# The last gated MLP on its selected rows alone: count, gather, compute, scatter

## What is computed

```python
def _L1_ffn_ref(x, attention_mask, wr, br, w1, b1, w2, b2):
    weights = (jnp.einsum('bsd,do->bso', x, wr) + br)[..., 0]
    k = max(1, int(CAPACITY * s))
    kk = k - 1 if k > 1 else 1
    _, idx = jax.lax.top_k(weights, k)
    sel_idx = idx[:, :kk]
    sel = jnp.take_along_axis(x, sel_idx[:, :, None], axis=1)
    h = jax.nn.gelu(jnp.einsum('bkd,dh->bkh', sel, w1) + b1)
    y = jnp.einsum('bkh,hd->bkd', h, w2) + b2
    w_sel = jnp.take_along_axis(weights, sel_idx, axis=1)
    y = y * w_sel[..., None]
    processed = jnp.zeros_like(x).at[batch_idx, sel_idx].set(y)
    return processed + x
...
x = x + _L1_ffn_ref(_layernorm(x, axis=-1)[None], ...)[0]
```

## Time and profile before

| | before |
|---|---|
| median of 3 runs, us | 9628.36 (9627.92 to 9630.96) |
| the profiled execution, us | 9602.17, of it a span of 9600.4 |
| norm3, from its first instruction to select's, us | 8602.9 to 8731.7 |
| select, us | to 8812.9 |
| ffn1, us | to 9560.6 |
| store, us | to the end of the span |

### The profile page before, as it was taken

One profiled execution on the slowest core, in us unless ns is written; L12 is line 12 of the kernel. 1 busy time (PEld: TensorE's weight loads), 2 busy tenths in 40 slices (PEclk: granted clock), 3 DMA queues, 4 the chain that ended last, 5 costly groups with the idle time before them and its releaser, 6 DMA issues. The chain is left out here.

```text
span 9600.4 us, 124500 instructions
## 1 busy us (share of the span) xinstructions
PE 6901.1 (72%) x33680; PEld 5343.1 (56%) x33681; DVE 3347.4 (35%) x5992; ACT 1650.1 (17%) x3477; POOL 4866.2 (51%) x6031
## 2 busy tenths in 40 slices
PE   2687776777756799766887888100498887886998
PEld 2544444555436576634666666100488886566886
DVE  4111113444323423333445454107333324992000
ACT  0123330000001122211222222000012332011221
POOL 1566657778772000476777777760365333651000
PEclk9898778899875899688889888655699998986999
DMA  4665555555432000356666666561689998861002
GB/s 147 230 201 176 182 171 186 170 170 173 128 91 80 25 20 22 128 186 199 198 200 199 201 196 201 184 189 35 191 285 305 305 305 280 277 215 56 17 19 65
DMA packets 724617, 1585.81 MB, mean 165 GB/s; under 512 B 135844, under 2 KB 442523, under 8 KB 691281
## 3 DMA queue, kind: packets, MB, share of 16 engines
q1 hardware_dynamic: 429272, 785.42, 24.5%
q0 software_dynamic: 206080, 553.05, 20.1%
q10 hardware_dynamic: 89115, 245.78, 7.0%
HBM read 1098.27 MB, written 487.90 MB: 165 GB/s over the span
## 5 line engine op out<-in xcount | busy, mean ns | idle before, releaser
L893 POOL DMA_INDIRECT rows_ring<-h_rows,src_idx x1660 | 1668.2, 1005 | 757.6 <-issue 474.2
L2627 POOL DMA_INDIRECT rows_ring<-x_rows,src_tile x1573 | 1543.3, 981 | 496.0 <-issue 432.0
L2290 PE MATMUL agg_ps_z<-agg_wt,agg_rows 128*128 128x110 f32 x8640 | 1043.3, 285 | 148.4 <-DVE agg_wt L2251 51.4
L2290 PEld LDWEIGHTS agg_ps_z<-agg_wt,agg_rows 128*128 128x128 f32 x8640 | 1027.4, 201 | 164.6 <-issue 164.4
L1014 PE MATMUL agg_ps_sum<-rows_ring,agg_sel_w 128*128 128x257 f32 x1960 | 645.9, 474 | 288.1 <-DMA rows_ring<-h_rows,src_idx 160.3
L2238 POOL DMA_DIRECT2D agg_rows<-tile_rows x864 | 465.8, 541 | 591.6 <-PE agg_ps_z L2290 522.0
L977 DVE TENSOR_TENSOR agg_sel<-iota,dst_item 128x640 bf16<-128x640 f32 x332 | 274.0, 825 | 916.3 <-PE agg_ps_sum L1015 647.7
L1014 PEld LDWEIGHTS agg_ps_sum<-rows_ring,agg_sel_w 128*128 128x128 f32 x1960 | 341.2, 218 | 445.1 <-issue 358.3
L1014 PE MATMUL agg_ps_sum<-agg_rows,agg_sel_w 128*128 128x257 f32 x1360 | 432.5, 462 | 153.9 <-issue 101.1
L2903 PE MATMUL mix_ps_h<-mix_x1t,mix_w 128*128 128x256 f32 x1600 | 395.6, 404 | 17.7 <-issue 8.5
L2912 PE MATMUL mix_ps_f<-mix_w,mix_ht 128*128 128x256 f32 x1600 | 389.0, 398 | 0.9 <-issue 0.9
(11 more groups left out here) (590 smaller groups left out, 12277.9 us busy)
## 6 DMA issues: line engine op xcount, KB each, us to landing
tile_rows<-rows_ring SPq DMA_DIRECT2D x121, 1696.5 KB
agg_rows<-tile_rows SPq DMA_DIRECT2D x1296, 128.0 KB
agg_rows<-tile_rows POOLq DMA_DIRECT2D x864, 128.0 KB
agg_rows<-edge_rows SPq DMA_DIRECT2D x68, 1290.0 KB
edge_rows<-rows_ring ACTq DMA_DIRECT2D x65, 1290.0 KB
z_sums<-agg_z ACTq DMA_DIRECT2D x98, 660.0 KB
fin_z<-z_sums SPq DMA_DIRECT2D x98, 660.0 KB
xn_turned<-norm_xt SPq DMA_DIRECT2D x200, 256.0 KB
```

The lines of the kernel that those rows point to most:

```text
L893: pool.indirect_dma_start(self.ring[:, lot % LOT_RING, i, :], None, self.table, bass.IndirectOffsetOnAxis(g.src_idx[:, item:item + 1], 0)) ...
L2290: mm = pe.matmul(ps[:, bass.ds(off + c * CW, CW)], rows[:, u, i, c * P:(c + 1) * P], wt[:, u, i, :, :].rearrange("p a b -> p (a b)"), star ...
L2627: pool.indirect_dma_start(self.ring[:, s, i, :], None, g.x_rows, bass.IndirectOffsetOnAxis(g.src_tile[:, tile:tile + 1], 0)).then_inc(self ...
```

## The change

The phases norm3, select, ffn1 and store become router, select and ffn1.

- **router** has no transposes and no matmul. DVE scales a group (two tensor_scalar) and then makes the router weight of each tile itself, by a scalar_tensor_tensor of `xn` and `wr` (both in SBUF) with the row sum as its accumulator output, two to a group. POOL adds `xn` into `x_sb` as before. SP stores the normalized group, and ACT stores x + n of the group, side by side into a DRAM table `slot_rows` (2 KB for each node: n in the first half, x + n in the second).
- **select** gets the seven stores of `x_sb` to the output, on SP, at its start. After the choice is made it builds tables: PE turns the 0/1 marks to one row for each tile, DVE scans them, and PE sums over tiles, so that `slot_counts` holds for each node how many are chosen up to it. For each of 6400 slots (`SEL_TILES` = 50 tiles of 128) DVE finds the tile that holds it, with a comparison of 128 x 5000 elements and a reduction over them.
- **ffn1** runs over 25 groups of slots, written out without a loop. POOL gathers, two indirect DMAs each for a group: the row of counts of each slot's tile, from which DVE counts the node (`find`); and that node's 2 KB row. PE transposes the group (4 transposes, `turn`), DVE copies it out of PSUM (`keep`) and makes the router weight again (`weigh`), PE and ACT do the MLP as before, DVE makes the result rows (`finish`), and POOL scatters them over the output by two indirect DMAs (`give`). Slots past the 6249th get a node number beyond the output, and their rows are dropped.
- store and `g.gain` are gone.

The core of the diff, cut:

```diff
@@ router (new) @@
+                for gi in range(GROUPS):
+                    u = gi % SLOTS
+                    if gi >= SLOTS:
+                        dve.wait_ge(rows_out[u], 16 * (gi // SLOTS))
+                        dve.wait_ge(added, gi + 1 - SLOTS)
+                        dve.wait_ge(weighed, GROUP * (gi + 1 - SLOTS))
+                    for j in range(GROUP):
+                        t = gi * GROUP + j
+                        dve.tensor_scalar(xn[:, u, j, :], g.x_sb[:, t, :], mean[:, t:t + 1], rstd[:, t:t + 1], ALU.subtract, ALU.mult).then_inc(scaled, 1)
+                    dve.wait_ge(scaled, GROUP * (gi + 1))
+                    if gi:
+                        dve.wait_ge(weighed, GROUP * gi)
+                    for j in range(GROUP):
+                        t = gi * GROUP + j
+                        dve.scalar_tensor_tensor(junk[:, j, :], xn[:, u, j, :], 1.0, wr[:, :], ALU.mult, ALU.mult,
+                                                 accum_out=g.router[:, t:t + 1]).then_inc(weighed, 1)
...
+                for gi in range(GROUPS):
+                    act.wait_ge(added, gi + 1)
+                    act.dma_start(table[gi, :, :, C:2 * C], g.x_sb[:, gi * GROUP:(gi + 1) * GROUP, :]).then_inc(base_out, 16)
...
+                    pool.wait_ge(scaled, GROUP * (gi + 1))
+                    at = g.x_sb[:, gi * GROUP:(gi + 1) * GROUP, :]
+                    pool.tensor_tensor(at, at, xn[:, gi % SLOTS, :, :], ALU.add).then_inc(added, 1)
...
+                    sp.wait_ge(scaled, GROUP * (gi + 1))
+                    sp.dma_start(table[gi, :, :, 0:C], xn[:, u, :, :]).then_inc(rows_out[u], 16)
@@ select @@
+                for a, b in zip(cuts[:-1], cuts[1:]):
+                    sp.dma_start(to[:, a:b, :], g.x_sb[:, a:b, :]).then_inc(stored, 16)
+                sp.dma_start(g.out[FULL_TILES * P:NODES, :], g.x_sb[0:TAIL, FULL_TILES, :]).then_inc(stored, 16)
+                sp.wait_ge(counts_ready, 1)
+                sp.dma_start(g.sel_counts, counts[:, :]).then_inc(stored, 16)
...
+                wide = [P, SEL_TILES, TILES]
+                done(dve.tensor_tensor(passed[:, :, :], ends[:, :].unsqueeze(1).to_broadcast(wide), g.slot_no[:, :].unsqueeze(2).to_broadcast(wide), ALU.is_le))
+                done(dve.tensor_reduce(tile_f[:, :], passed[:, :, :], AX, ALU.add))
@@ ffn1, POOL @@
+                def ask_counts(gi):
+                    s = gi % SEEN
+                    if gi >= SEEN:
+                        pool.wait_ge(found, gi - SEEN + 1)
...
+                def ask_rows(gi):
+                    s = gi % HELD
+                    pool.wait_ge(found, gi + 1)
+                    if gi >= HELD:
+                        pool.wait_ge(added, gi - HELD + 1)
...
+                        pool.indirect_dma_start(rows[:, s, j, :], None, g.sel_rows, bass.IndirectOffsetOnAxis(row_at[:, k:k + 1], 0)).then_inc(held[s], 16)
...
+                def give(gi):
+                    s = gi % OUT
+                    pool.wait_ge(added, gi + 1)
...
+                ask_counts(0)
+                ask_counts(1)
+                for gi in range(N):
+                    if gi + 2 < N:
+                        ask_counts(gi + 2)
+                    ask_rows(gi)
+                    if gi >= 3:
+                        give(gi - 3)
+                for gi in range(N - 3, N):
+                    give(gi)
@@ ffn1, PE @@
+                turn(0)
+                for gi in range(N):
+                    u = gi % 2
+                    pe.wait_ge(kept, gi + 1)
+                    for i in range(4):
...
+                    if gi + 1 < N:
+                        turn(gi + 1)
+                    if gi:
+                        last(gi - 1)
+                last(N - 1)
@@ ffn1, DVE @@
+                find(0)
+                find(1)
+                dve.wait_ge(w_loaded, 96)
+                keep(0)
                 b2.split(dve, g)
+                weigh(0)
+                for gi in range(N):
+                    if gi + 2 < N:
+                        find(gi + 2)
+                    if gi + 1 < N:
+                        keep(gi + 1)
+                        weigh(gi + 1)
+                    if gi:
+                        finish(gi - 1)
+                finish(N - 1)
```

More of the change, by code:

```diff
@@ L77 @@
 KEEP = NODES // 2 - 1
+SEL_TILES = -(-KEEP // (2 * P)) * 2
 TERMS = GAT_HEADS + 1
@@ L3208, in _, with turn @@
             @block.tensor
             def _(pe):
-                pe.wait_ge(w_loaded, 64)
-                pe.wait_ge(b2.ready, 1)
-                def last(gi, u, first):
+                pe.wait_ge(w_loaded, 96)
+                def turn(gi):
+                    pe.wait_ge(held[gi % HELD], 16 * GROUP * (gi // HELD + 1))
+                    if gi:
+                        pe.wait_ge(kept, gi)
+                    for j in range(GROUP):
+                        for c in range(KC):
+                            mm = pe.transpose(ps_t[:, c, j * P:(j + 1) * P], rows[:, gi % HELD, j, c * P:(c + 1) * P], g.ident[:, :])
+                    mm.then_inc(turned, 1)
```

261 lines of the change are left out of this document (186 added, 75 removed).

## The result

The changed kernel takes **9229.0 us** (median of 4 runs, 9227.5 to 9279.1), the kernel before 9629.7 (4 runs, 9627.9 to 9647.0): ratio 0.959, 95% interval 0.9571 to 0.961. The prediction was 9282 with a range of 9238 to 9328.

The account below looks back on a forecast made before the run. PE was taken to bound ffn1 from end to end; -382.4 (ffn1 and store) + 14.8 (tables) + 21.7 (router) = -345.9 us, taking the median 9628.4 to 9282.5 us, range 9238 to 9328.

Parts of the forecast that it names:

- What bounds, and the halved work: ffn1: PE stays the bound, 25 groups replace 50, and ffn1 with store falls from 787.5 to 405.1 us, gain 382.4.
- first result: ffn1: 14.8 us of start, then 25.7 us from first matmul to first result, 40.5 us in all.
- 22 periods of 15.23: ffn1: each group costs today's 14.63 us plus 0.6 for four transposes; 22 such periods make 375.6 us.
- The start: ffn1's start: POOL's eight indirect DMAs (9.8 us), landing 2.6, transposes 1.1, copy 0.7 and waits 0.6 make 14.8 us.
- The store: Seven output stores beside select: their 39.8 us fit into its 81.2 us without DMA, so cost nothing.
- The tables: select's end: a serial chain with two long operations of 5.3 us each, cost 14.8 us, range 13 to 20.
- Router: router for norm3: POOL's addition holds DVE's second sum, period 2.85 us, stage 150.5 us against 128.8, cost 21.7.
- A: router: no contention, DVE's sums run beside POOL's addition, period 2.0 us, 42 us less, total 9241; chance 8%.
- B: ffn1: a handover in each group costs 1 to 2 us more, 25 to 50 in all, 9308 to 9333; chance 13%.
- C: ffn1: run-ahead fails, gathers asked for only when due, 30.9 us a group, 392 us more, 9675; chance 2%.
- D: ffn1: work not halved, as slots past the choice were many, near 9650 with the tables' cost; under 1%.
- The carry-over: Whole kernel: the profiled execution's 26.2 us under the median of runs carried over, 9628.4 - 345.9 = 9282.5 us.

Follow-up runs that it names:

- r8: Changed kernel over 100 tiles of slots in place of 50 (50 groups, the last 25 without selected nodes), on the second chip: 9410.5 us, ratio 1.0034 against the kernel before.
- r3: Changed kernel with the seven output stores behind the counts' store, at select's end and not its start: 9262.8 us, ratio 0.962 against the kernel before.
- r1: Changed kernel with POOL's addition of n into x_sb left out in router, stores kept: 9189.8 us, ratio 0.954 against the kernel before.
- r4: Changed kernel with POOL giving out results of group gi-2 in place of gi-3 before the next gathers: 9387.4 us, ratio 0.9745 against the kernel before.
- r10b: Changed kernel with x + n on ACT, ffn1's weights loaded in select, tables cut in two, first rows asked for earlier; third chip: 8981.2 us.
- r15: Changed kernel with eight memsets ahead of the bisection's loop, on the fourth chip: 9299.8 us, ratio 0.9574 against the kernel before.
- r13: Changed kernel with its two new DRAM tensors declared last, on the fourth chip: 9292.7 us, ratio 0.9573 against the kernel before.

## Why the prediction was right and wrong

**What bounds, and the halved work: right.** ffn1 went from 747.7 to 407.7 us with the scatters in it, PE never waited but at the start, and r8 shows that 25 groups are worth 384 us. The sum's terms for ffn1 and store: first result 40.5 forecast, 42.9 measured (8862.7 from 8819.8); 22 periods of 15.23, measured 15.07, 3.6 us less, as a turn costs 0.44 and not 0.6; the tail from the last result to the end 7.2 forecast, 10.9 measured. Three misses of 2 to 4 us that cancel to +2.6.

**The start: wrong path, 2.9 us too short.** The first half began 17.7 us into the phase and not 14.8. I had taken eight indirect DMAs on POOL as the path, and the landing of the earlier trace rows, 2.6 us, as that of the counts too. It took 6.3 us beside the 2 MB of weights, and 2.0 without them. The mis-sized term is the landing in company.

**The store: right.** It cost nothing at select's head, and 27 us at its end (r3).

**The tables: right.** Both long operations came within 0.1 us of 5.3, and the chain came to 14.7 against 14.8. What select took beyond that is the bisection's 0.1 us per pass, a step the prediction does not have, since nothing in that loop's source changes.

**Router: the contention right, the period mis-sized.** 2.52 and not 2.85 us; over 49 periods that is 16.2 of the 18.5 us by which the stage fell short (132.0 against 150.5). The step that failed is the sum "0.73, 0.05, 0.42 with 0.08, 1.27, 0.28 and 0.08 plus three semaphore waits": the period is 0.73 for the scalings, 0.04, 0.35 to the second sum's start, and 1.40 from there to the next scaling. The accumulator is read beside the next operation, the waits are already met, and POOL's addition begins 0.04 us after the first sum, not behind it. (It takes 1.50 us and not 1.27, which gives part of this back.) I had the material for that: "2.8 if the first sum comes first" counted the first sum and the whole addition one after the other, and 2.85 was then chosen between two cases that both added waits. The Trainium skill, page SBUF — State Buffer, section SBUF: two separate sides, calls the shared port pair an exclusive lock that goes to whichever starts first; the trace agrees, with the first sum at 0.43 us, the second at 1.48 and 0.42 once the addition is gone (r1). Its consequence as I had put it, the first sum winning by 0.04 us, is what happened.

**The rivals.** A is out, as the second sum takes 1.48 us. Its time, 9241, was nearly reached for other reasons. B is out: 15.07 per group leaves no room for a handover. C did not come, and r4 shows how near its place was: one `give` earlier, and PE waits in each group. D is out by r8.

**The carry-over: wrong.** "I carry that difference over" took the profiled run's 26 us below the median as a fixed property. The kernel before was profiled in an execution faster than all its others shown here (9602 against 9614 to 9648), and the kernel after had no such offset. Why that one execution was faster no trace shows. Together with the 15 us of untouched phases, 12 of which are the second gather loop's (5 to 17 us between any two traces on one chip), this is 41 of the 53 us. It depends on the chip: on the second and third the same change is worth 353 to 364 us in medians, within 18 of the forecast 346. The range failed on this, as it held only costs of the change and nothing for the 8600 us that it leaves alone or for the choice of the execution. Either miss alone, router's 16 us or these 41, is larger than the 9 us by which the range was missed.

## What to carry to other kernels

Price a stage by the operation that is late next, in one period written out with start times: operations that overlap at issue and waits that are already met must not be added. Give POOL a two-input addition beside DVE's two-input work only where both have time to spare; a scaling with a bias on an idle ACT did the same for 40 us less. And when a change touches a tenth of the span, leave a few tenths of a per cent in the range for the rest of it: with the same source, one loop ran 5 to 17 us faster in the changed program, and another 46 to 73 us faster on one chip and 3 to 14 slower on two others.

## What the runs showed of the hardware

- A gather of 512-byte rows issued beside a 2 MB load was used 6.3 us after its issue ended, and 2.0 us when the load was moved away (r10b).
- An indirect gather that POOL issued while DVE ran a two-input operation of 4.74 us took 5.00 us to issue in place of 1.05; beside a one-input reduction of 4.73 us it took 0.94 (r10b).
- With a PE wait of 4.5 us in each 22 us the granted clock was 0.87 where it is 1.00 without it (r4), and the 16 matmuls behind the wait took 5.1 to 6.2 us where 3.7 is usual.
- The same loop took 2.23 or 2.34 us a pass, with and without eight short instructions ahead of it (r15, r13), and the same indirect gather 973 or 981 ns, 1005 or 1015, on the mean in two builds.
- Stores of 256 KB, two for each group, reached 351 GB/s (r1), above the 322 of the 2 MB stores in the earlier trace rows.
- The kernel before took 9380, 9389, 9630 and 9706 us on four chips.
